# Group-norm statistics through DRAM instead of two small matmuls, in a channel-attention kernel

## What is computed

```python
g = x.reshape(B, 32, 12, H, W)                       # group norm, 32 groups of 12 channels
xn = (g - mean(g, (2, 3, 4))) / sqrt(var(g, (2, 3, 4)) + 1e-5)
w = einsum('bnc,oc->bno', tokens(xn), qkv_w)         # 12 heads of 32 channels
wn = w / max(sqrt(sum over n of w*w), 1e-12)
Pi = softmax over heads of (sum over d of wn*wn) * temp
Pi_n = Pi / (sum over n of Pi + 1e-8)
attn = 1 / (1 + einsum('bhn,bhnd->bhd', Pi_n, w*w))
out = einsum('bnc,oc->bno', -(w * Pi) * attn, out_w) + out_b
y = x + out
```

## Time and profile before

| | |
|---|---|
| Runs | median 917.19 us of 3 (916.14 to 918.69) |
| The profiled execution | 916.16 us |
| Its span in the profile | 914.3 us |
| Granted TensorE clock, mean | 0.991 |
| Busy: PE, DVE, ScalarE, POOL | 878.0, 720.4, 541.5, 225.5 us |
| HBM read and written | 102.24 and 51.92 MB |
| DMA queue q1 (SyncE): packets, share of 16 engines | 36672, 46.7% |

### The profile page before, as it was taken

The page is one execution under the profiler, slowest core; times in us unless marked ns, Lnnn a source line. Parts: engine busy times, 40 slices in busy tenths (PEclk is TensorE's granted clock), DMA queues, the critical chain, the costliest instruction groups (busy, mean ns, idle before and its releaser), DMA issues.

```text
span 914.3 us, 14405 instructions
## 1 busy us (share of the span) xinstructions
PE 878.0 (96%) x4404; PEld 691.1 (76%) x4404; DVE 720.4 (79%) x1366; ACT 541.5 (59%) x740; POOL 225.5 (25%) x101
## 2 busy tenths in 40 slices
PE   4699999999999999999999999999999999999976
PEld 3568777777877777877777787777787777778754
DVE  7478877888887787887788888878788778888654
ACT  3465656765566675565676555667556567655621
POOL 1122333212333321233321233332123332113300
PEclk9899999999999999999999999999999999999997
DMA  7125544445544345554445554434555444454331
GB/s 270 58 72 209 189 162 153 154 185 207 209 151 180 132 170 204 209 189 161 154 148 187 207 209 147 186 133 170 200 209 185 164 156 148 185 207 142 141 140 70
DMA packets 36836, 154.39 MB, mean 169 GB/s; under 512 B 4306, under 2 KB 7762, under 8 KB 32850
## 3 DMA queue, kind: packets, MB, share of 16 engines
q1 hardware_dynamic: 36672, 154.17, 46.7%
q10 hardware_dynamic: 146, 0.00, 0.0%
HBM read 102.24 MB, written 51.92 MB: 169 GB/s over the span
## 4 chain that ended last, share of the span: by engine, by line
PE 93%; DVE 3%; DMA 1%; issue 1%; ACT 1%; DVEq 0%; SPq 0%; ACTq 0%
PE acc L466 86%; PE scores L546 5%; PE scores L554 1%; DVE stats L626 1%; DMA PIB<-pi 1%; DVE WS L729 1%; PE small L454 0%; DMA X<-in_x 0%; PE small L460 0%; DVE XL L676 0%; DVE UL L765 0%; PE acc L443 0%; DVE X L773 0%; ACT XH L393 0%; DVE WV L755 0%
## 5 line engine op out<-in xcount | busy, mean ns | idle before, releaser
L317 POOL TENSOR_TENSOR XL<-XN,XH 128x1024 fp32r<-128x1024 f32 x93 | 222.5, 2408 | 623.3 <-ACT XH L393 623.3
L365 ACT ACTIVATE WS<-acc 128x1024 f32<-128x1024 f32 x96 | 98.7, 1028 | 275.0 <-PE acc L466 274.7
L466 PE MATMUL acc<-UH,W2H 128*128 128x512 f32 x576 | 181.4, 398 | 7.9 <-ACT UH L355 7.9
L773 DVE SCALAR_TENSOR_TENSOR X<-acc,bias,X 128x1024 f32<-128x1024 f32 x96 | 118.3, 1260 | 85.8 <-PE acc L466 85.8
L466 PE MATMUL acc<-XH,W1H 128*128 128x512 f32 x576 | 183.9, 401 | 2.0 <-ACT XH L393 2.0
L466 PE MATMUL acc<-XH,W1L 128*128 128x512 f32 x576 | 180.6, 395 | 0.0
L466 PE MATMUL acc<-UH,W2L 128*128 128x512 f32 x576 | 180.2, 396 | 0.0
L466 PE MATMUL acc<-UL,W2H 128*128 128x512 f32 x576 | 150.3, 396 | 0.0
L466 PE MATMUL acc<-XL,W1H 128*128 128x512 f32 x576 | 147.0, 390 | 0.5 <-POOL XL L317 0.5
L466 PEld LDWEIGHTS acc<-UL,W2H 128*128 128x128 f32 x576 | 105.7, 188 | 33.8 <-issue 12.8
L466 PEld LDWEIGHTS acc<-UH,W2H 128*128 128x128 f32 x576 | 106.5, 190 | 29.5 <-ACT UH L355 8.5
(11 more groups left out here) (74 smaller groups left out, 469.6 us busy)
## 6 DMA issues: line engine op xcount, KB each, us to landing
PIB<-pi SPq DMA_DIRECT2D x96, 516.0 KB, 6.3
out_y<-X SPq DMA_DIRECT2D x96, 512.0 KB, 7.4
X<-in_x SPq DMA_DIRECT2D x31, 1536.0 KB, 6.3
pi<-PIT SPq DMA_DIRECT2D x32, 48.4 KB, 1.6
X<-in_x SPq DMA_DIRECT2D x3, 512.0 KB, 4.8
WV<-in_L_conv_qkv_w SPq DMA_DIRECT2D x1, 576.0 KB, 6.7
WS<-in_L_conv_out_w SPq DMA_DIRECT2D x1, 576.0 KB, 7.7
temp_row<-in_L_conv_temp ACTq DMA_DIRECT2D x1, 0.0 KB
```

The lines of the kernel that those rows point to most:

```text
L317: pool.tensor_tensor(XL[:, t, :], XN[:, t, :], XH[:, t, :].bitcast(F32), ALU.subtract).then_inc(xl_done, 1)
L365: act.activation(square_tile(i, t), acc[:, t, :], ACT.Square, accum_out=sumsq[:, t:t + 1]).then_inc(squared, 1)
L466: last = pe.matmul(out[:, h * BANK:(h + 1) * BANK], w[:, k, m * P:(m + 1) * P], r[:, k, h * BANK:(h + 1) * BANK], start=(n == 0 and k == 0 ...
L773: dve.scalar_tensor_tensor(x_tile(j, t), acc[:, t, :], bias[:, t:t + 1], x_tile(j, t), ALU.add, ALU.add).then_inc(y_done, 1)
```

## The change

Image 0 keeps the old way, under the names `first_group_...`, with a semaphore of its own and a copy of the two results from PSUM into the new tile `group_mv`. For images 1 to 31 the two matmuls, the offset and the spread go. Instead, SyncE writes the raw `stats` (36 floats per partition, 18 KB) to a DRAM tensor and reads them back so that each of the four partitions of a group gets all its 144 floats (`gathered`, 72 KB). DVE aggregates those into the group's mean and variance, `group_mv`. The write stands on SyncE's queue between the PIB reads and the first store, the gather behind the second store; the aggregation stands on DVE where `group_spreads` stood, one step later than the old `group_moments`. A gather waits until the write has landed.

```diff
+        gathered = sb("gathered", [P, PER_GROUP * T * HALVES * 6])
+        group_mv = sb("group_mv", [P, 2])
...
+        stats_dram = nc.dram_tensor("stats_rows", [P, T * HALVES * 6], F32).ap()
...
+            def write_stats(j):
+
+                if has(j):
+                    sp.wait_ge(gn_step, j.counts(GN_STEPS, GN_MEASURED))
+                    if j.follows(2):
+                        sp.wait_ge(stats_gathered, j.counts(16, -16))
+                    sp.dma_start(stats_dram, stats[:].rearrange("p k s -> p (k s)")).then_inc(stats_written, 16)
+
+            def gather_stats(j):
+
+                if has(j):
+                    sp.wait_ge(gn_step, j.counts(GN_STEPS, GN_AGGREGATED - GN_STEPS))
+                    sp.wait_ge(stats_written, j.counts(16))
+                    rows = stats_dram.rearrange("(g k) s -> g (k s)", k=PER_GROUP).unsqueeze(1)
+                    sp.dma_start(gathered[:], rows.to_broadcast([GROUPS, PER_GROUP, PER_GROUP * T * HALVES * 6]))\
+                        .then_inc(stats_gathered, 16)
...
                 spread_pi(i)
+                write_stats(i + 2)
                 store(i - 1, 0)
                 store(i - 1, 1)
-
+                gather_stats(i + 2)
+
+            write_stats(FIRST + 1)
+            gather_stats(FIRST + 1)
             pipeline(sp, step, 0, B + 1)
...
-                    act.wait_ge(gn_step, j.counts(GN_STEPS, GN_VARIANCES))
-                    act.activation(log_var[:], variances_of(j), ACT.Ln, bias=gn_eps[:]).then_inc(gn_step, 1)
+                    act.wait_ge(gn_step, j.counts(GN_STEPS, GN_AGGREGATED))
+                    act.activation(log_var[:], group_mv[:, 1:2], ACT.Ln, bias=gn_eps[:]).then_inc(gn_step, 1)
...
-            def group_means(j):
...
-            def group_variances(j):
...
+            def first_group_sums():
...
                 first_product(i, 0)
-                group_means(i + 1)
                 first_product(i, 1)
                 first_product(i, 2)
-                group_variances(i + 1)
                 second_product(i - 1, 0, {(2, 0): lambda: head_sums(i)})
...
+                if j.follows(2) and tiles[0] == 0:
+                    dve.wait_ge(stats_written, j.counts(16, -16))
                 for t in tiles:
...
+                dve.wait_ge(first_gn, FIRST_VARIANCES)
+                dve.tensor_copy(group_mv[:], small[:, 0:2]).then_inc(gn_step, 1)
...
             def group_moments(j):
...
+                if has(j):
+                    dve.wait_ge(stats_gathered, j.counts(16))
+                    dve.memset(wait_cell[:], 0.0)
+                    dve.bn_aggr(group_mv[:], gathered[:]).then_inc(gn_step, 1)
...
                     attention(i - 1, k)
-                group_spreads(i + 1)
+                group_moments(i + 1)
                 weigh(i - 1, 0)
...
                 group_stats(i + 2, range(1, T))
-                group_moments(i + 2)
                 finish(i - 1, 0)
                 finish(i - 1, 1)
```

More of the change, by code:

```diff
@@ L41 @@
 QUAD = 32
-(GN_MEASURED, GN_AGGREGATED, GN_MEANS, GN_OFFSET, GN_SPREAD, GN_VARIANCES, GN_LOGGED, GN_SEEDED, GN_SCALED, GN_RESIDUE,
- GN_ROOTED, GN_STEPS) = range(1, 13)
+(GN_MEASURED, GN_AGGREGATED, GN_LOGGED, GN_SEEDED, GN_SCALED, GN_RESIDUE, GN_ROOTED, GN_STEPS) = range(1, 9)
+FIRST_AGGREGATED, FIRST_MEANS, FIRST_OFFSET, FIRST_SPREAD, FIRST_VARIANCES = range(1, 6)
 HEADSUM_STEPS = 3
@@ L181, in conv_attention @@
         weights_lo = sem("weights_lo")
+        first_gn = sem("first_gn")
         gn_step = sem("gn_step")
+        stats_written = sem("stats_written")
+        stats_gathered = sem("stats_gathered")
         xn_done = sem("xn_done")
@@ L220, in norm_of @@
             return norm[:, j.slot % 2, 0:1], norm[:, j.slot % 2, 1:2]
[L222 to L228, removed]
         def w_tile(j, t):
@@ L444, in turn_weights @@
                     last.then_inc(weights_turned, 1)
-            def group_means(j):
[L448 to L454, removed]
-            def group_variances(j):
-                if has(j):
-                    pe.wait_ge(gn_step, j.counts(GN_STEPS, GN_SPREAD))
-                    pe.matmul(variances_of(j), group_mean[:], spread[:], start=True, stop=True).then_inc(gn_step, 1)
+            def first_group_sums():
+                pe.wait_ge(groups_set, 2)
+                pe.wait_ge(first_gn, FIRST_AGGREGATED)
+                pe.matmul(small[:, 0:1], group_mean[:], part_mv[:, 0:1], start=True, stop=True).then_inc(first_gn, 1)
+                pe.wait_ge(first_gn, FIRST_SPREAD)
+                pe.matmul(small[:, 1:2], group_mean[:], spread[:], start=True, stop=True).then_inc(first_gn, 1)
             def term(out, m, left, right, n, k):
@@ L574, in _ @@
             pe.matmul(temp_ps, ones[0:1, :], temp_row[0:1, :], start=True, stop=True).then_inc(temp_spread, 1)
-            group_means(FIRST)
-            group_variances(FIRST)
+            first_group_sums()
             pe.wait_ge(masks_step, 3)
@@ L628, in group_stats, with first_group_moments, first_group_spreads @@
                         last.then_inc(gn_step, 1)
-            def group_moments(j):
[L632 to L639, removed]
+            def first_group_moments():
+                dve.wait_ge(gn_step, GN_MEASURED)
+                dve.bn_aggr(part_mv[:], stats[:].rearrange("p k s -> p (k s)")).then_inc(first_gn, 1)
+            def first_group_spreads():
+                dve.wait_ge(first_gn, FIRST_MEANS)
+                dve.tensor_scalar(offset[:], small[:, 0:1], part_mv[:, 0:1], None, ALU.subtract).then_inc(first_gn, 1)
+                dve.wait_ge(first_gn, FIRST_OFFSET)
+                dve.tensor_scalar(spread[:], offset[:], offset[:], part_mv[:, 1:2], ALU.mult, ALU.add)\
+                    .then_inc(first_gn, 1)
+                dve.wait_ge(first_gn, FIRST_VARIANCES)
+                dve.tensor_copy(group_mv[:], small[:, 0:2]).then_inc(gn_step, 1)
+            def group_moments(j):
                 if has(j):
[L642 to L645, removed]
+                    dve.wait_ge(stats_gathered, j.counts(16))
+                    dve.memset(wait_cell[:], 0.0)
+                    dve.bn_aggr(group_mv[:], gathered[:]).then_inc(gn_step, 1)
             def group_norm(j):
@@ L651, in group_norm @@
                     dve.wait_ge(gn_step, j.counts(GN_STEPS, GN_SEEDED))
-                    dve.tensor_scalar(scaled[:], variances_of(j), GN_EPS, seed[:], ALU.add, ALU.mult).then_inc(gn_step, 1)
+                    dve.tensor_scalar(scaled[:], group_mv[:, 1:2], GN_EPS, seed[:], ALU.add, ALU.mult).then_inc(gn_step, 1)
                     dve.wait_ge(gn_step, j.counts(GN_STEPS, GN_SCALED))
@@ L660, in group_norm @@
                     dve.wait_ge(gn_step, j.counts(GN_STEPS, GN_ROOTED))
-                    dve.tensor_scalar(shift_j, means_of(j), -1.0, rstd_j, ALU.mult, ALU.mult).then_inc(gn_step, 1)
+                    dve.tensor_scalar(shift_j, group_mv[:, 0:1], -1.0, rstd_j, ALU.mult, ALU.mult).then_inc(gn_step, 1)
             def normalise_first():
@@ L814, in _ @@
             dve.tensor_reduce(temp_o[:], pick[:], AX_X, ALU.add).then_inc(temp_kept, 1)
-            group_moments(FIRST)
-            group_spreads(FIRST)
+            first_group_moments()
+            first_group_spreads()
             group_norm(FIRST)
@@ L825, in _ @@
             group_stats(FIRST + 1, range(T))
-            group_moments(FIRST + 1)
             pipeline(dve, step, 0, B + 1)
```

## The result

The changed kernel takes 908.19 us (median of 4, 906.31 to 908.83), beside 916.71 for the kernel before (median of 4: the three of the table above and one more). The ratio is 0.990, with a 95% interval of 0.9878 to 0.9921. It is faster by about 1%, and 1.0 us from the forecast of 907.2. The profiled execution took 908.83 us with a span of 907.0.

The account below looks back on a forecast made before the run. TensorE (PE) was taken as the bound; without two matmuls a step, the gather wait leaves 0.31 us over 29 intervals (-9.0), ends -1: -10 on 916.16 gives 906.2, plus 1.03 to the median, 907.2 us; range 894 to 928.

Parts of the forecast that it names:

- The wait for the gather: DVE ahead of the aggregation: gather lands at 433.45, DVE waits from 432.17, so head sums come 26.71 us apart.
- PE's own period: PE in steady images: 26.30 us without the matmuls, read from the last head-sum interval, which has no next image.
- It lies 0.72 below 27.02, of which the two matmuls explain 0.67: Last head-sum interval against the steady one: nearly all the difference was put down to PE's two removed matmuls.
- Rival A: Gather hidden, landing by 433.05; PE's 26.30 decides, saving 0.72 an image, total 895.3 us; chance 0.22.
- PE by itself would be ready after 26.30 [...] and 0.31 of the 0.72 remain: PE at the head sums: stands 0.4 us a step for DVE's weights, leaving 0.31 us gain an image.
- The ends: First step, opening chain and head sums 0 to 1: -1 us in all, between -2.5 and +1.
- the foreseen 1 us for the late gather: Head sums 0 to 1, no stores queued: gather still lands about 1 us after DVE asks for it.
- The rule from the Trainium skill: Each DMA costs about 2.0 us fixed: write lands at 432.2, gather at 434.2, total 929 us.
- rival B: Serial write and gather round trip: gather lands at 434.5, interval 27.76, total 937.7 us; all later landings 0.23.
- point of decision: Gather landing at 433.75, 0.3 us past the forecast value, beyond which the slower serial round trip decides.
- SyncE blocked, the late load: SyncE holds the third store to about 431.4, load goes out about 435.0; costs nothing, over 1 us to spare.

Follow-up runs that it names:

- n3: Changed kernel with only ScalarE's seeds of the next image moved ahead of the square of tile 2, DMA order unchanged; 902.69 us, 0.9846 of the kernel before.
- n2: e1 with ScalarE's seeds of the next image ahead of the square of tile 2, turn_pi still at (1, 1); 891.92 us, 0.9729 of the kernel before.
- b1: Control: the kernel before with only turn_pi moved on PE from (1, 1) to (1, 2); 910.55 us, 0.9931 of the kernel before.
- n1: e1 with turn_pi moved on PE from (1, 1) to (1, 2); 892.19 us, 0.9731 of the kernel before.
- e1: Changed kernel with the statistics write ahead of the PIB reads and the gather ahead of the stores; 905.90 us, 0.9877 of the kernel before.
- e2: Changed kernel, both DMAs issued, but DVE aggregates its own partition's 36 floats without waiting for the gather; 905.28 us, 0.9871 of the kernel before.
- e6: Changed kernel with only the gather moved ahead of the first two stores, write still behind the PIB reads; 907.81 us, 0.9895 of the kernel before.
- e7: The kernel before, in step 0 alone with image 1's group means after tile 1 instead of tile 0; 912.74 us, 0.9951 of the kernel before.
- e5: Changed kernel with one unread matmul of the old shape put back after tile 0 in steps 1 to 30; 914.99 us, 0.9978 of the kernel before.

## Why the prediction was right, and where it was not

The time was right within 1 us, and its range and direction held. Its parts held in unequal measure.

**The wait for the gather: right, up to the head sums.** The prediction's chain, counted from the head sums at 415.14 there and 410.94 in the changed trace: gather issued at +15.61, measured +15.40; landed at +18.31, measured +18.10 (426.34 + 2.7); start of weigh at +18.81, measured +18.90; next head sums at +26.71, measured +26.80. Two terms were off and offset each other. The write took only 0.2 us behind the PIB reads instead of 0.5, and the aggregation of 144 floats took 0.80 instead of 0.45. DVE's wait was 0.94 us an image ((31.9 - 3.8) / 30), not 1.3. The last step agrees partly by luck. DVE's weights were ready at +26.49. The prediction gave 0.08 from there to the head sums; where PE does wait it takes 0.27 (n3: 434.11 + 0.26 to 434.64), which makes +26.76. In this image PE came a little later still, held up by the turn, and did not wait for the weights. Over the 29 intervals PE stood 0.22 us an image for the head sums and not the forecast 0.4; the other 0.30 above 26.30 is the stop at the turn. n3, where little but this loop is left, gives 26.66.

**PE's own period: the landmark was right, its reading wrong.** 26.30 is reached, by n2. But the step "It lies 0.72 below 27.02, of which the two matmuls explain 0.67" failed. The last interval has its `turn_pi` at (1, 1) like the others, but PE finds PI ready there. DVE has no statistics of a further image to make ahead of the softmax. In image 14 they stand at 415.93 and the softmax begins at 417.13, 1.99 us behind the start of the head sums. In image 30 it begins 1.58 behind it, when the head sums are done, and the weight load of `turn_pi` has no wait. From the kernel before:

```profile
415.93 1.28 DVE L626 BATCH_NORM_STATS2 stats<-X 128x6 f32<-128x512 f32 x2
...
417.13 0.45 DVE L700 STREAM_TRANSPOSE scores<-scores 128x256 f32<-128x256 f32 x1
...
848.88 0.47 DVE L700 STREAM_TRANSPOSE scores<-scores 128x256 f32<-128x256 f32 x1 [1.02 <-PE scores L546]
...
851.38 0.12 PEld L554 LDWEIGHTS scores<-identity,PI 128*96 128x96 f32 x1
```

So the last interval is free of two things, the matmuls and the stop. It points at a remedy that no run tried: the softmax ahead of the first tile of the statistics. By b1 and n1 the 0.71 between 27.00 and 26.3 are 0.20 of stop at the turn and some 0.5 of matmuls, 0.26 each.

**Rival A (895.3): its condition came true, its time did not.** In e1, e2 and e6 the gather is hidden, and the time is 905 to 908. The matmul removed behind tile 2 had filled PE's time before `turn_pi`; without it the stop there grows from 0.2 to 0.5 us. That stop, and not the gather, is what keeps 26.77 from falling further. In the changed kernel the two bounds lie side by side, 26.66 through the gather and 26.77 through the turn, and the kernel runs at 26.82, a little over both, since images differ in which of the two is the longer. So the forecast's 0.31 us an image became 0.18: the step "PE by itself would be ready after 26.30 [...] and 0.31 of the 0.72 remain" was mis-sized. The turn alone would already have held it at 26.77, and the prediction had no term for it.

**The ends: mis-sized the other way.** Forecast -1, measured -2.04 (-3.80 + 1.19 + 0.08 + 0.49). The head start is larger because the stop in step 0 also cost PE its clock for 3.4 us. From head sums 0 to 1 the changed trace takes 1.19 longer. That looks like the foreseen 1 us for the late gather, but it isn't shown to be that. e7 has no gather and gives back 1.44 there (26.60 against 25.16), and the changed trace has 3.4 us more of the low clock in this stretch.

That the total came within 1 us is luck in part. An error of 3.7 us in the intervals (-9.0 forecast, -5.3 measured) meets one of 1 us the other way in the ends, which leaves 2.7 in the profiled pair: it differs by 7.3 us where 10 were forecast. The scatter of the executions hides most of that. The profiled execution lies 1.03 below the median in the kernel before and 0.64 above it in the changed one, and the ratio says 9.

**The rule from the Trainium skill.** The Trainium skill, "DMA: Bandwidth & Descriptors" (its part on the anatomy of one DMA), has about 2.0 us of fixed cost for a DMA. That part is on DMAs issued by GpSimd, and those here are issued by SyncE. In an idle queue this case agrees roughly (gather 2.2 us in e6, write of the statistics 1.4 at its fastest). Behind other transfers it does not: the write landed 0.2 us after the PIB read in front of it, with rows of 144 bytes. Here the measurement decides, and rival B (937.7) falls with the rule: its point of decision was a landing at +18.61, and the gather landed at +18.10.

**SyncE blocked, the late load:** as forecast. The third store goes out at 427.10 and the load at 430.59, and no new wait for X appears.

**The best version.** n2_early_seeds computes the same and takes 891.92 us, 0.9729 of the kernel before. By the traces the change makes it possible: the group's variance no longer waits for a matmul behind tile 2, so the seeds can be taken where ScalarE is idle. No run tried early seeds without the change.

## What to carry to other kernels

Work taken off the bounding engine is worth its time only outside the stretches in which that engine would wait anyway; look for them at its weight loads and in the chain that ended last, and test them by putting one piece back at a time. A small transfer in a busy queue costs the queue in front of it more than its own size (6.2 us here for 18 KB): issue it ahead of the large ones. A landmark from the last trip of a loop must be checked for everything else that is different there. And before a chain of waits is called confirmed, look whether its last step really waited.

## What the runs showed of the hardware

- `bn_aggr` took 0.31 us for 36 floats and 0.80 for 144, 4.5 ns a float; `bn_stats` takes 0.68 us for 512 (about 1.3 ns each).
- A float32 matmul of 128 x 128 weights with one column costs PE 0.26 us in the stream, though the weight loads around it move apart by 0.33 (e5 against e1; b1 against n2, half of 0.51).
- A DRAM write of 18 KB landed 0.2 us behind the transfer ahead of it (changed kernel) and 1.4 us after its issue in an idle queue.
- A stop of 1.85 us on PE near the start was followed by 3.4 us at 0.51 of the clock, and one of 3.5 us at the first `turn_pi` by another 3.4 us in the kernel before and some 6.8 in the changed one; in the steady part of the changed kernel, with stops of some 0.3 us and the longest 1.25, it stayed at 1.00 (window 60 to 880 us).
